# Two narrow attentions: the product with the values of a key tile issued once, over all its queries, in every second period

## What is computed

```python
x = x + _L0_attn_ref(_layernorm(x), ...)    # 16 heads of 16, causal, rotary positions
x = x + _L0_xattn_ref(_layernorm(x), ctx, ctx, mask, ...)
x = x + _L0_ffn_ref(_layernorm(x), ...)     # 8 experts, one per token
x = x + _L1_attn_ref(_layernorm(x), ...)    # 16 heads of 64
x = x + _L1_xattn_ref(_layernorm(x), ctx, ctx, ...)
x = x + _L1_ffn_ref(_layernorm(x), ...)     # self-attention, 16 heads of 16, then 8 experts, two per token
```

```python
scores = jnp.einsum('bqhd,bkhd->bhqk', q, k) * scale
probs = jax.nn.softmax(scores, axis=-1)          # the first one with a causal mask
out = jnp.einsum('bhqk,bkhd->bqhd', probs, v)
```

## Time and profile before

| | us |
|---|---|
| median of 3 runs | 2835.51 |
| lowest, highest | 2833.72, 2842.75 |
| profiled execution, own time | 2831.68 |
| its span in the profile | 2829.8 |
| stage a0, first to last exponential | 275.5 |
| stage a5, first to last exponential | 368.5 |
| a regular group of a0, of a5 | 32.8, 45.0 |

### The profile page before, as it was taken

The page is one execution under the profiler, slowest core; times in us unless marked ns, Lnnn a source line. Parts: engine busy times, 40 slices in busy tenths (PEclk is TensorE's granted clock), DMA queues, the critical chain, the costliest instruction groups (busy, mean ns, idle before and its releaser), DMA issues. The chain is left out here.

```text
span 2829.8 us, 44855 instructions
## 1 busy us (share of the span) xinstructions
PE 2418.5 (85%) x16004; PEld 1293.2 (46%) x16010; DVE 1618.0 (57%) x2605; ACT 1130.6 (40%) x2043; POOL 1046.2 (37%) x818
## 2 busy tenths in 40 slices
PE   5678997876998995999999999778759999967998
PEld 4523334235886773333333333542522222246887
DVE  4778874655333333566666664237668999743222
ACT  2436664331000331444444444123426777721221
POOL 2521003312443112677777777112350000004665
PEclk8879998557998997999999999875868999978999
DMA  4432212426775555122222221442352121036665
GB/s 140 113 79 62 74 28 79 110 81 164 233 204 154 179 190 187 45 87 65 87 83 83 72 84 50 130 110 70 89 130 56 32 62 31 9 97 175 200 187 151
DMA packets 222332, 301.58 MB, mean 107 GB/s; under 512 B 54138, under 2 KB 164756, under 8 KB 221655
## 3 DMA queue, kind: packets, MB, share of 16 engines
q1 hardware_dynamic: 180886, 226.29, 25.8%
q0 software_dynamic: 36800, 68.23, 10.4%
q10 hardware_dynamic: 4480, 4.88, 0.9%
HBM read 200.87 MB, written 97.76 MB: 106 GB/s over the span
## 5 line engine op out<-in xcount | busy, mean ns | idle before, releaser
L1623 ACT ACTIVATE a_probs<-a_cols 128x512 f32<-128x512 f32 (+3 forms) x896 | 445.2, 549 | 244.6 <-PE a_cols L1553 164.9
L1645 DVE TENSOR_REDUCE a_mxw<-a_rows 128x2 f32<-128x1024 f32 (+1 forms) x448 | 475.5, 1099 | 68.5 <-PE a_rows L1511 43.1
L2072 DVE TENSOR_REDUCE a_mxw<-a_rows 128x2 f32<-128x1024 f32 x256 | 313.3, 1224 | 208.2 <-PE a_rows L1910 206.4
L2050 ACT ACTIVATE a_probs<-a_cols 128x1024 f32<-128x1024 f32 x256 | 261.6, 1024 | 267.3 <-PE a_cols L1939 252.0
L1891 POOL TENSOR_TENSOR a_sums<-a_sums,a_probs 128x1024 f32<-128x1024 f32 x128 | 309.3, 2417 | 100.6 <-ACT a_probs L2050 87.3
L1553 PE MATMUL a_cols<-a_qs,a_ks 50*128 50x512 bf16 (+7 forms) x1792 | 276.8, 365 | 15.2 <-DMA a_qs<-a_nparts 8.8
L2346 PE MATMUL e_psU<-e_xT,e_w 128*128 128x256 f32 x1216 | 272.3, 383 | 6.9 <-DMA e_b<-in_b 6.2
L1935 PE MATMUL a_cols<-a_qf,a_kf 64*128 64x512 f32 x1024 | 266.7, 599 | 0.0
L1581 PE MATMUL a_out<-a_probs,a_vs 128*17 128x256 f32 (+4 forms) x3328 | 257.5, 383 | 0.2 <-ACT a_probs L1623 0.2
L2346 PEld LDWEIGHTS e_psU<-e_xT,e_w 128*128 128x128 f32 x1216 | 233.2, 192 | 40.0 <-issue 6.8
L1511 PE MATMUL a_rows<-a_ks,a_qs 48*128 48x512 bf16 (+3 forms) x896 | 174.4, 386 | 89.5 <-DVE a_mxw L1645 43.1
(11 more groups left out here) (282 smaller groups left out, 3423.6 us busy)
## 6 DMA issues: line engine op xcount, KB each, us to landing
e_w<-in_w SPq DMA_DIRECT2D x69, 512.0 KB, 5.5
e_w<-in_w SPq DMA_DIRECT2D x30, 1024.0 KB, 8.0
a_qs<-q_scratch SPq DMA_DIRECT2D x336, 64.0 KB, 2.3
qk_wide_scratch<-t_f SPq DMA_DIRECT2D x32, 512.0 KB, 2.9
q_scratch<-t_parts POOLq DMA_DIRECT2D x56, 192.0 KB, 2.6
a_ks<-k_scratch SPq DMA_DIRECT2D x144, 64.0 KB, 2.4
vw_scratch<-t_v SPq DMA_DIRECT2D x8, 1040.0 KB, 4.6
a_vs<-vw_scratch SPq DMA_DIRECT2D x16, 520.0 KB, 6.7
```

Source lines behind the costliest of these rows:

```text
L1623: act.activation(pr[ug % RING][:, 2 * hp + e, c0:512], psC[(2 * at + e) % 3][:, 0:512 - c0], ACT.Exp, scale=scale).then_inc(ex_done, 1)
L1645: dve.tensor_reduce(mxw[w][:, a, hp, :, t % 4:t % 4 + 1], src[:, :, 0:n], AX.X, ALU.max).then_inc(s_free, 1)
L2050: act.activation(pr[i][:], psC[i % 2][:], ACT.Exp, scale=scale).then_inc(ex_done, 1)
L2072: dve.tensor_reduce(mxw[:, j % 2, :, j // 2:j // 2 + 1], psR[:], AX.X, ALU.max).then_inc(s_free, 1)
```

## The change

In `values` the cut into parts goes. The odd period (`part` 0) now issues nothing for any unit; the even period issues the product of the whole unit, from `c0` to 512, for each of the four heads, and signals `pv_done` as before. Every unit is thereby treated as the unit i = 0 was. Nothing else is edited: the plan, the order of the slots, the scores, the exponentials, DVE and the DMAs are the same.

```diff
-                    if part == 0 and i == 0:
+                    if part == 0:
                         return
-                    if part == 0 or i == 0:
-                        pe.wait_ge(ex_done, (g * NUG + ug + 1) * H)
+                    pe.wait_ge(ex_done, (g * NUG + ug + 1) * H)
                     if i == 0:
                         wait(pe, o_turned, 2 * g + w)
-                    mid = (c0 + 512) // 2
-                    a, b = (0, 512) if i == 0 else (c0, mid) if part == 0 else (mid, 512)
                     for h in range(H):
-                        mm = pe.matmul(psO[32 * h:32 * h + VC, a:b], vs[p][:, i, h, :], pr[ug % RING][:, h, a:b],
-                                       start=i == 0, stop=ug + 1 == unit_end[w] and part == 1)
-                    if part == 1:
-                        mm.then_inc(pv_done, 1)
+                        mm = pe.matmul(psO[32 * h:32 * h + VC, c0:512], vs[p][:, i, h, :], pr[ug % RING][:, h, c0:512],
+                                       start=i == 0, stop=ug + 1 == unit_end[w])
+                    mm.then_inc(pv_done, 1)
```

## The result

The change made the kernel slower: 2900.11 us median (2894.85 to 2906.04, 4 runs) against 2839.13 us of the kernel before, a ratio of 1.0217 with a 95% interval of 1.0184 to 1.0249. Forecast was 2892 us in a range of 2866 to 2918. The profiled execution took 2894.85 us, its span is 2893.0 us, 63.2 more than before.

The account below looks back on a forecast made before the run. PE was taken to bound both stages, with merging stalling it on three score buffers. 37 us in a5 plus 19 in a0 gave +56 on a median of 2835.5, so 2892 us, range 2866 to 2918.

Parts of the forecast that it names:

- What bounds: Both stages: PE sets the pace, busy 43.2 of 45.0 us in a regular a5 group, DVE close behind at 42.3.
- Does it repeat: Merged a5 units: the i = 0 stall recurs in every unit, a closed loop of 3.03 us instead of 2.63.
- What the change saves: Value product on PE: one of 512 queries for two of 256 saves 0.14 us a unit, 27 us over 192 units.
- rival 1: Score buffers in both stages: three suffice, PE stays full and saved product work decides, 2809 us; chance 0.04.
- a5 by group: Stage a5: +5.0 us for groups 1 to 6, +2.5 for group 0, +5 for the last; sum 37 us.
- a relief: DVE's output turnings in a5, twice a group: slack lowers each one's cost from roughly 0.7 to about 0.4 us.
- PE's waits for it at the rows steps nearly gone: Sign expected in a regular a5 group's profile: PE hardly waits for DVE at rows steps, DVE's busy share down to 0.85.
- a0 by group: Stage a0: +2.6 us for groups 1 to 6, +1.5 for group 0, +2.3 for the last; sum 19 us.
- the three waits for DVE that I had named: PE in a0, 320.5 to 329.0 us: waits of 0.41, 0.72 and 0.63 us for DVE's reductions; merged units there cost nothing.
- DVE hid almost nothing: Rival 2, a5 rows steps: DVE's waits hide most stalls; half hidden +28, 2863 us, nearly all within 0.3%; chance 0.14.
- The clock fell: Rival 3, both stages: PE's stalls lower the granted clock; at mean 0.93, 44 us more, 2936 us; chance 0.09.
- The sum: Both stages: 37 us in a5 plus 19 in a0, +56 us, median 2892 us, +2.0%.

Follow-up runs that it names:

- the fourth buffer: Four score buffers instead of three in a5, one-head rows steps over half of the keys: merged in a5 2774.69 against 2834.46 us, halves 2794.77 against 2803.39.
- the last experiment: Kernel before, but in a5 one-head rows steps over half of the keys, four score buffers and the merged product: 2774.69 us, ratio 0.9777.
- the four last experiments: Kernel before with one-head rows steps over half of a5's keys; three buffers: halves 2803.39, merged 2834.46 us; four: halves 2794.77, merged 2774.69.
- all four kernels with one row buffer: Kernel before with rows steps of at most 256 keys, one row buffer; three score buffers: halves 2867.82, merged 2958.50 us; four: 2856.52, 2878.50.
- the kernel with the rows steps in the gap: Against the change: in a5 the rows step of each odd period is run in the even period after it; 2895.03 us, 1.0196 of the kernel before.

## Why the prediction held

- **What bounds.** Right. The decisive step was to read the i = 0 unit as a sample of the new order: 3.03 us there, 3.03 in the ordinary units after.
- **Does it repeat.** Right; the loop of 0.63 + 0.54 + 0.11 + 0.54 + 0.98 + 0.23 has the score buffer as its cause, as the fourth buffer showed in a5, with rows steps of one head.
- **What the change saves.** Too small, and read wrongly. "The 0.14 is what does not depend on the width" is true, but it belongs to the visit to a product, not to the number of matmuls (0.99 us for 16 records, 0.98 for 8), and 0.09 us ahead of the product go with it: PE is spared 0.22 us a unit, 42 us in 192 units and not 27. The forecast did not suffer, since 3.03 us was read whole from the i = 0 unit; rival 1's 2809 us and the 2.49 us expected of the last experiment did. The estimate from "TensorEngine Tiling (Array Packing)", section Instruction Overhead in the Trainium skill, 0.2 us for eight records fewer, is not borne out: the trace shows 0.01. That the whole saving of 0.22 us has the size of that estimate is chance, since it does not come from the number of records. The same page's Key Properties in the Trainium skill, by which a change of the tiling mode drains the engine, would fit, since the scores load 50 x 128 and the product 128 x 17; no run here separates a drain from other costs of going over.
- **a5 by group.** 5.2 us against 5.0. The parts were right: ten of the 14 merged units rose from 2.63 to 3.03 us, two with two rows steps from 3.03 to 3.46, and the two behind a turning from 3.33 to 3.46, a relief of 0.27 where I had 0.3. The sign "PE's waits for it at the rows steps nearly gone" did not come: after a turning PE waits 0.89 us for DVE (0.63 before), only it no longer waits for ACT in the same unit. Group 0 was +0.2 instead of +2.5, and +2.0 against a run with the old code at nearly the same clock. My reading of group 0, half waits for transfers and half clock, was wrong: PE waited 1.8 us for a transfer and 2.8 for DVE, and was busy for 51.9 us instead of 43.2. The last was +5.3 instead of +5.
- **a0 by group.** 2.3 against 2.6, groups 0 and 1 +3.5 and +3.3 where I had +1.5 and +2.6. That the sum of 20.6 came near 19 is in part luck. Of group 0's 3.5 us some may be clock, 0.77 after and 0.86 before: in the four last experiments, which leave a0 as it was, group 0 took 47.4 and 47.7 us at 0.86 and 0.85, and 49.4 and 49.9 at 0.74 and 0.73; yet the kernel merged in a0 only took the change's 51.1 at 0.70. In a regular group the last of the three waits for DVE that I had named ends 17.6 us after the group's first exponential, where it ended after 17.3 before. So 0.3 of the 2.3 us arise up to there and 2.0 behind it. That the merged units beside these waits cost nothing was right, but the units ahead of them cost almost nothing either, where I had a price for them. Two of the three waits stayed as said, 0.72 and 0.63 us (below); the first went from 0.41 to 0.75, and PE's waits for DVE in the group from 2.5 us to 3.7. What each unit of the second half costs was not worked out:

```profile
338.95 0.28 PE L1511 MATMUL a_rows<-a_ks,a_qs 48*128 48x256 bf16 x2 [0.72 <-DVE a_mxw L1641]
...
341.36 0.39 PE L1511 MATMUL a_rows<-a_ks,a_qs 48*128 48x512 bf16 x2 [0.63 <-DVE a_mxw L1641]
```

- **Rivals.** With four score buffers less work on PE does pay, with three it does not. DVE hid almost nothing in regular groups of a5, 0.27 us at each turning. The clock fell in no regular group of the profiled execution; PE's idle times there had not been "0.6 us and less" before, as I wrote, but up to 0.72. In kernels beside this one it did fall in regular groups of a0: to 0.91 once with the product in the odd period (36.0 us for 33.6), and to between 0.80 and 0.96 in all four kernels with one row buffer.
- **The sum.** 56 us forecast, 57.4 in the two stages, 61.0 between the medians, 63.2 between the spans. The median of 2900.11 lies 8 us over the 2892: about 4 of that is the kernel before itself, 2839.13 with a fourth execution instead of 2835.5; the rest fits the 6 us elsewhere and the executions with a lower clock, which the runs do not separate.

## What to carry to other kernels

Work that stands between two fills of a small ring of buffers is also the time in which the ring empties; before products are gathered into fewer, longer ones, count the buffers against the consumer's time in the stretch that is left bare. If the kernel already contains one instance of the new order, at a loop's first pass or last, its rows are the first estimate. And a test that frees a resource by taking another has to be read for the wait that this creates.

## What the runs showed of the hardware

**A visit to a product has a fixed cost of about 0.22 us on PE**, 0.09 ahead of its first record and 0.13 behind it, and inside a product the cut does not matter: above, 16 records against 8, and a unit of 1.96 us against 2.19.

**A rows step of one head runs beside a score matmul**: both start at 2271.83, where a rows step of two heads delays the scores by 0.23 us.

**The clock at the end of a0.** The code of a0 is the same in the change and in the kernel with the rows steps in the gap. Its last group ran at full clock in the one profiled execution and at 0.60 in the other:

```profile
429.50:458.00 28.50, 23.96 (x256) 7.69 (x248) 4.22 (x8) 20.88 (x48) 1.91 (x4) 1.00 0.06 11
```

```profile
430.70:470.70 40.00, 36.42 (x256) 9.10 (x252) 4.21 (x8) 20.94 (x48) 1.92 (x4) 0.60 0.04 8
```

That is 11.5 us for the same instructions. Of the four executions of the change two have a mean clock of 0.903 (2894.85 and 2896.32 us) and two of 0.893 and 0.894 (2903.91 and 2906.04); the difference of 9 to 10 us fits such a group, but their traces were not kept, so where it arose is inferred. With the product in the odd period the last group of a0 ran at 0.67 and took 36.6 us, PE busy for 32.3. In the kernel with short rows steps, three buffers and merged products, all of a0 ran at a mean of 0.81 and took 343.1 us, in halves at 0.84 and 315.5. Before the change the last group of a0 ran at 1.00 with PE busy for 25.3 of 26.2 us; merged it is 24.0 of 28.5. What starts the fall is open.
